# One core's fused image tokenizer, attention and expert block: the token product of the coming pair issued earlier on TensorE, into another bank, with the shared products and VectorE's list reordered

## The reference, cut to what matters

```python
tokens = einsum('bsd,hd->bsh', patches, W) + b      # 196 patches of 588 values
h = concat([cls, tokens], 1) + pos; h = concat([h, txt], 1)
x = layernorm(h)
...
total = gate * total + (1.0 - gate) * pos_contrib   # causal sums over the sequence
h = h + x + total / norm @ Wo + bo
x = layernorm(h)
scores = sigmoid(x @ gate_w.T)                      # top 2 of 64 experts, 256 places each
routed = sum over the 2 experts of (silu(x w1) * (x w3)) w2 * weight
shared = (silu(x @ sw1) * (x @ sw3)) @ sw2
h = h + shared + routed
```

## Time and profile before

| what | value |
|---|---|
| runs of the kernel before | 1828.45, 1853.2, 1863.95 us (median 1853.2) |
| profiled execution, first to last instruction (its span; no other time of that execution is listed) | 1823.6 us |
| TensorE matmul busy, share of the span | 84% |
| VectorE, ScalarE, GpSimd busy | 78%, 69%, 67% |
| mean granted TensorE clock | 0.956 of full |

### The profile page before, as it was taken

One profiled execution on the slowest core, in us unless ns is written; L12 is line 12 of the kernel. 1 busy time (PEld: TensorE's weight loads), 2 busy tenths in 40 slices (PEclk: granted clock), 3 DMA queues, 4 the chain that ended last, 5 costly groups with the idle time before them and its releaser, 6 DMA issues.

```text
span 1823.6 us, 30829 instructions
## 1 busy us (share of the span) xinstructions
PE 1534.0 (84%) x9237; PEld 1158.6 (64%) x9237; DVE 1421.6 (78%) x5705; ACT 1256.5 (69%) x2195; POOL 1226.0 (67%) x973
## 2 busy tenths in 40 slices
PE   2888998999899999888989898999889975676672
PEld 1566776777676767656767666677667764554552
DVE  3477997999797988777888888889888975587661
ACT  2897997988788878777878787889878851111110
POOL 1025776777676767666667676777667767488887
PEclk9899999999999999999999999999999998899886
DMA  9965666666666666556555655566656221476653
GB/s 182 229 138 120 138 139 125 123 121 124 102 117 100 117 101 106 96 103 103 95 101 104 108 102 102 101 111 105 103 103 103 63 59 40 96 116 109 98 88 35
DMA packets 267117, 197.21 MB, mean 108 GB/s; under 512 B 65464, under 2 KB 246437, under 8 KB 266953
## 3 DMA queue, kind: packets, MB, share of 16 engines
q1 hardware_dynamic: 210120, 174.84, 50.2%
q0 software_dynamic: 51200, 17.87, 8.4%
q10 hardware_dynamic: 5633, 2.56, 0.7%
HBM read 86.24 MB, written 85.39 MB: 94 GB/s over the span
## 4 chain that ended last, share of the span: by engine, by line
PE 40%; ACT 22%; issue 11%; POOL 9%; another core or an unknown queue 8%; DVE 7%; DMA 3%; SPq 0%; ACTq 0%; POOLq 0%; DVEq 0%
POOL out_rows L639 6%; PE bank L919 5%; PE bank L999 5%; ACT img L656 5%; ACT xh L739 4%; PE bank L1087 3%; PE bank L982 3%; POOL slot_rows L605 3%; PE bank L946 2%; PE bank L1018 2%; PE bank L1078 2%; ACT xs L726 2%; ACT kq L793 2%; ACT kq L792 2%
## 5 line engine op out<-in xcount | busy, mean ns | idle before, releaser
L605 POOL DMA_INDIRECT slot_rows<-xs,slot x768 | 874.1, 1138 | 284.5 <-issue 247.3
L656 ACT ACTIVATE img<-img 84x980 f32<-84x980 f32 x190 | 339.6, 1788 | 14.8 <-DMA img<-in_x 7.2
L591 POOL TENSOR_TENSOR rs<-ve,neg_half 128x12 f32<-128x12 f32 (+1 forms) x66 | 150.3, 2277 | 234.4 <-DVE ve L1342 232.8
L919 PE MATMUL bank<-img,w_tok 126*128 126x392 f32 (+1 forms) x640 | 228.7, 505 | 27.9 <-DMA img<-img 23.3
L639 POOL DMA_INDIRECT out_rows<-img,etok x128 | 198.7, 1552 | 64.0 <-issue 35.0
L919 PEld LDWEIGHTS bank<-img,w_tok 126*128 126x128 f32 (+1 forms) x640 | 124.0, 195 | 113.3 <-issue 23.3
L982 PEld LDWEIGHTS bank<-pos_a,v 128*128 128x128 f32 x768 | 145.4, 198 | 54.0 <-issue 10.8
L982 PE MATMUL bank<-pos_a,v 128*128 128x325 f32 (+2 forms) x768 | 163.8, 351 | 6.1 <-issue 3.8
L726 ACT ACTIVATE xs<-h,nb,rs 128x128 f32<-128x128 f32 x384 | 154.0, 481 | 3.0 <-DVE nb L1348 3.0
L739 ACT ACTIVATE xh<-h,nb,rs 128x128 f32<-128x128 f32 x384 | 154.0, 480 | 1.3 <-DVE nb L1348 1.3
L1499 DVE TENSOR_TENSOR h<-bank,hbo 128x768 f32<-128x768 f32 x64 | 61.1, 955 | 114.6 <-remote 103.3
(11 more groups left out here) (217 smaller groups left out, 3697.1 us busy)
## 6 DMA issues: line engine op xcount, KB each, us to landing
img<-in_x SPq DMA_DIRECT2D x384, 150.1 KB
img<-img SPq DMA_DIRECT2D x254, 160.8 KB
img<-img SPq DMA_DIRECT2D x128, 128.6 KB
out_rows<-fin SPq DMA_DIRECT2D x128, 128.0 KB
slot_rows<-xs,slot POOLq DMA_INDIRECT x768
slot_rows<-init_rows SPq DMA_DIRECT2D x16, 540.0 KB, 9.1
img<-slot_rows SPq DMA_DIRECT2D x32, 270.0 KB
h<-in_txt SPq DMA_DIRECT2D x64, 128.0 KB
```

What stands on the lines that cost most here:

```text
L591: g.tensor_tensor(out=rs[:, q.u, half:], in0=ve[:, q.u, half:], in1=neg_half[:, half:], op=ALU.pow).then_inc(S["p_rs"], 1)
L605: g.indirect_dma_start(out=slots_d, out_offset=bass.IndirectOffsetOnAxis(ap=slot[0:nt, q.x, r, part:part + 1], axis=0), in_=xs[0:nt, q.x, ...
L656: a.activation(cols[:, b0:b0 + nb, :], raw[:, q.u, :].rearrange("p (t b) -> p b t", b=P)[:, b0:b0 + nb, :], ACT.Copy)\
L919: ins = mm(bank[:, 5, 0:2 * PATCHES], w_tok[r, m, :], xk[r, k.u, :, m, :], start=(m == 0), stop=(m == SHIFT - 1))
```

## The change

- On TensorE `token(k)` moves from behind the shared products to right behind `position_out_1(p2)`. It writes bank 3 instead of bank 5, and waits for ScalarE's `angles` of pair k-2 (`a_th`), the reader of bank 3, instead of its gate.
- `shared_1a` and `shared_1b` come next, in that order, then `position_out_0`, then `shared_3a` and `shared_3b` into banks 4 and 5 (they were 3 and 4). The waits move with them: `shared_1a` waits for `v_h2`, `shared_3a` for `v_fin` and the gate, and `pe_f1a` (which ScalarE's SiLU waits for) is counted by `shared_1b`.
- `shared_out` waits for a new semaphore `v_su`, which `shared_product` counts, instead of `v_ht`. `products(w)` counts the pairs whose shared products are not put off. Where no further pair runs (the end of the first part) `shared_1a` and `counts` get a wait of their own.
- On VectorE `token_sum` moves in front of `block_pairs` and `score`; `weigh_position` moves from behind `indices` to behind `score`, and `shared_product` behind it, so that these two stand last before `residual_bias`.

No instruction with work in it is added or removed. The diff, cut to its core:

```diff
@@ token
-                wait(pe, S["a_g"], k, 2)
+                wait(pe, S["a_th"], k, 2)
...
-                    ins = mm(bank[:, 5, 0:2 * PATCHES], w_tok[r, m, :], xk[r, k.u, :, m, :],
+                    ins = mm(bank[:, 3, 0:2 * PATCHES], w_tok[r, m, :], xk[r, k.u, :, m, :],
@@ shared_out
-                wait(pe, S["v_ht"], w, -4)
                 if later(w):
                     tr(bank[:, 4, 0:TILE], ident, ident).then_inc(S["pe_o"], 1)
                     return
+                pe.wait_ge(S["v_su"], products(w))
@@ shared_1a
+                wait(pe, S["v_h2"], z, -1)
...
+                if not later(z):
+                    mm(bank[:, 0, 0:L], sw1[:, :], x2_t[:, 0, :], start=True, stop=True)
@@ shared_1b
-                wait(pe, S["v_h2"], z, -1)
...
+                    mm(bank[:, 1, 0:L], sw1[:, :], x2_t[:, 1, :], start=True, stop=True).then_inc(S["pe_f1a"], 1)
@@ shared_3a
+                    wait(pe, S["v_fin"], z, 1)
+                    wait(pe, S["a_g"], z, -2)
+                    mm(bank[:, 4, 0:L], sw3[:, :], x2_t[:, 0, :], start=True, stop=True)
@@ TensorE's body
                     gates(p2)
                     position_out_1(p2)
+                if k.runs():
+                    token(k)
+                    if first(k):
+                        position_products()
                 if p4.runs():
+                    shared_1a(p4)
                     shared_1b(p4)
                 if p2.runs():
                     position_out_0(p2)
                 if p4.runs():
                     shared_3a(p4)
                     shared_3b(p4)
-                    shared_1a(p4)
-                if k.runs():
-                    token(k)
-                    if first(k):
-                        position_products()
                 if p2.runs():
                     scores(p2)
@@ VectorE's body
                     indices(p4)
-                if p2.runs():
-                    weigh_position(p2)
                 if p4.runs():
                     one_hot(p4)
                     score_low(p4)
...
                 if p4.runs():
                     either(p4)
-                    shared_product(p4)
+                if k.runs():
+                    token_sum(k)
+                if p4.runs():
                     block_pairs(p4)
                     score(p4)
-                if k.runs():
-                    token_sum(k)
+                if p2.runs():
+                    weigh_position(p2)
+                if p4.runs():
+                    shared_product(p4)
                 if p2.runs():
                     residual_bias(p2)
```

More of the change, by code:

```diff
@@ L143, in first, with products @@
     return pair.c == 0
+def products(pair):
+    return pair.count() - sum(c <= pair.c for c in LATER)
 def steps(body, begin, end):
@@ L396, in program @@
              v_max v_lohi v_imax v_idx v_hot v_both v_bp v_cnt v_pick v_place v_over v_slot v_fin
-              v_sg  v_sinv
+              v_sg  v_sinv v_su
             a_d0 a_d1 a_d2 a_h a_xh a_xt a_th a_abs a_sin a_qs a_g a_x2 a_x2t a_lgt a_sl a_lg a_small
@@ L966, in counts @@
                 pe.wait_ge(S["v_bp"], w.count())
+                if not w.back(-2).runs():
+                    pe.wait_ge(S["a_sl"], w.count())
                 flat = both[:, :, :].rearrange("p t e -> p (t e)")
@@ L1021, in shared_3b @@
             def shared_3b(z):
-                wait(pe, S["v_fin"], z, 1)
-                wait(pe, S["a_g"], z, -2)
                 if later(z):
-                    tr(bank[:, 4, 0:TILE], ident, ident).then_inc(S["pe_f3b"], 1)
+                    wait(pe, S["v_fin"], z, 1)
+                    wait(pe, S["a_g"], z, -2)
+                    tr(bank[:, 5, 0:TILE], ident, ident).then_inc(S["pe_f3b"], 1)
                 else:
-                    mm(bank[:, 4, 0:L], sw3[:, :], x2_t[:, 1, :], start=True, stop=True).then_inc(S["pe_f3b"], 1)
+                    mm(bank[:, 5, 0:L], sw3[:, :], x2_t[:, 1, :], start=True, stop=True).then_inc(S["pe_f3b"], 1)
             def shared_1a(z):
[L1032 to L1035, removed]
+                wait(pe, S["v_h2"], z, -1)
+                if not z.back(-1).runs():
+                    wait(pe, S["v_fin"], z, 1)
+                if not later(z):
+                    mm(bank[:, 0, 0:L], sw1[:, :], x2_t[:, 0, :], start=True, stop=True)
             def logits(z):
@@ L1044, in shared_1b @@
             def shared_1b(z):
-                wait(pe, S["v_h2"], z, -1)
-                if not later(z):
-                    mm(bank[:, 1, 0:L], sw1[:, :], x2_t[:, 1, :], start=True, stop=True)
+                if later(z):
+                    tr(bank[:, 0, 0:TILE], ident, ident).then_inc(S["pe_f1a"], 1)
+                else:
+                    mm(bank[:, 1, 0:L], sw1[:, :], x2_t[:, 1, :], start=True, stop=True).then_inc(S["pe_f1a"], 1)
             def shared_3a(z):
                 if not later(z):
-                    mm(bank[:, 3, 0:L], sw3[:, :], x2_t[:, 0, :], start=True, stop=True)
+                    wait(pe, S["v_fin"], z, 1)
+                    wait(pe, S["a_g"], z, -2)
+                    mm(bank[:, 4, 0:L], sw3[:, :], x2_t[:, 0, :], start=True, stop=True)
             def transpose_1(k):
@@ L1352, in token_sum @@
                 dve.wait_ge(S["pe_tok"], k.count())
-                TT(h_t[:, :, 1:NIMG], bank[:, 5, 0:2 * PATCHES].rearrange("p (s t) -> p s t", s=2),
+                TT(h_t[:, :, 1:NIMG], bank[:, 3, 0:2 * PATCHES].rearrange("p (s t) -> p s t", s=2),
                    pos_t[:, 1:NIMG].rearrange("p (o t) -> p o t", o=1).to_broadcast([D, 2, PATCHES]), ALU.add)\
@@ L1485, in shared_product @@
                 if not later(z):
-                    TT(su[:, :, :], sl[:, :, :], bank[:, 3:5, 0:L], ALU.mult)
+                    TT(su[:, :, :], sl[:, :, :], bank[:, 4:6, 0:L], ALU.mult).then_inc(S["v_su"], 1)
             def top_values(z):
```

## The result

The changed kernel takes 1925.35 us (median of 4 runs, 1912.65 to 1936.81), the kernel before beside it 1857.35 us (4 runs, 1828.45 to 1863.95). The ratio is 1.043, with a 95% interval of 1.033 to 1.054: slower by 68 us where 38 were forecast. Ratios and their intervals leave out executions in a slower state of the chip, so a ratio is not the quotient of the two medians beside it. The profiled execution of the changed kernel has a span of 1923.2 us, 99.6 us more than that of the kernel before (1823.6); the two profiles lie further apart than the medians. Lines have moved: L924 is the token product (L919 before), L965 the scores (L960), L1510 the second sum (L1499), L1471 `weigh_position` (L1460), L1364 the token sum (L1353), L1089 the projection (L1078), L463 the spreads (L458).

What follows compares the result with a forecast made beforehand. TensorE (matmuls 92% busy in a middle stretch) and VectorE (85%) were taken to bound the kernel. Terms of 30 and 8 us gave 38, added to 1853.2: 1891 us, slower by 2.1%; range 1835 to 1935.

Steps and rivals of the forecast that it cites:

- L1048's idle time: TensorE's wait for the second sum before its first shared product, 30.2 us over the program; forecast to vanish.
- 25 pairs, 30 us: Token product in prompt pairs: waits 1.4 us for its patches, scores 1.4 us later; 1.2 us taken in 25 pairs.
- prompt: Pairs whose second sum on VectorE has no "remote" wait, 25 of 64; TensorE was said to have no gap there.
- late pair: One of 39 of 64 pairs whose second sum has a "remote" wait; the token product was to fill 2.29 us of waiting.
- The landing: Time from SP's last spread issue to the patches being there: 3.1 us, from one token product released by the DMA.
- remote: VectorE's wait before the second sum, 103.3 us, read as TensorE's counts coming late while SP issues; forecast near 100 us.
- rival A: Late counts before the second sum shrink: 60 us less, 1793 us, faster; sign "remote" under 60 us; chance 0.14.
- Scores 8.7 us behind the sum in late pairs: Forecast sign in the profile after: scores, waiting for `weigh_position`, start at 8.7 us instead of 7.80.
- forecast shift of 0.9 us: TensorE reaches its next projection 0.9 us later in late pairs, as scores wait for `weigh_position` in VectorE's new order.
- This VectorE step: VectorE's new order in late pairs: costs 0 to 0.9 us in each of 39, 0.2 taken, 8 us.
- B: Rival: no change; patches land by 906, the 0.9 us stays hidden behind SP; 8 us or less, about 1858; chance 0.26.
- C: Rival: much slower; patches land after 5 us, not 3.1, prompt pairs pay 3.3 us; 75 us, 1928 us; chance 0.14.

Runs made afterwards that it cites:

- before, profiled again: The kernel before, unedited, run and profiled again beside the experiments: 1793.87 us, ratio 1.00.
- after, profiled again: The changed kernel, unedited, run again beside the experiments: 1900.06 us, ratio 1.060 to the kernel before.
- wait filled: The changed kernel with three spare products on TensorE ahead of the token product's wait for its patches: 1841.28 us, ratio 1.027 to the kernel before.
- two of three early: The changed kernel with the spreads of the first two column chunks issued ahead of the store, the last chunk's behind it: 1850.97 us, ratio 1.033.
- early patches: The changed kernel with the third column chunk turned ahead of the shared SiLU and all spreads issued ahead of the store: 1808.44 us, ratio 1.009.
- token back, weigh first: The changed kernel with the token product in its old place and `weigh_position` ahead of the token sum, now behind `score`: 1800.89 us, ratio 1.001.
- `weigh_position` first: The changed kernel with early patches, and `weigh_position` ahead of `token_sum`, `block_pairs` and `score` on VectorE: 1809.58 us, ratio 1.006 to the kernel before.

## Why the prediction was wrong in its size

The pair, cut at VectorE's finished rows, the second sum and the scores, means over 55 pairs of the middle, worked out from the starts and ends in each timeline ("rows" are the finished rows, the end of `add_shared`):

| us per pair | rows to sum | sum to scores | scores to next rows | pair |
|---|---|---|---|---|
| before, first runs | 8.32 | 8.30 | 6.02 | 22.64 |
| after, first runs | 6.70 | 11.85 | 5.71 | 24.26 |
| before, profiled again | 7.42 | 8.66 | 5.92 | 22.00 |
| after, profiled again | 6.84 | 11.65 | 5.44 | 23.93 |
| wait filled | 6.22 | 11.20 | 5.54 | 22.96 |
| two of three early | 6.06 | 10.48 | 6.51 | 23.05 |
| early patches | 6.04 | 9.74 | 6.44 | 22.22 |
| token back, weigh first | 7.22 | 8.85 | 5.76 | 21.83 |

**Right.** The sign, the place and the releaser: the token product waits for its patches in the new place, TensorE's list behind it is late, and the scores come later behind the sum. The early patches take the wait away, and with it 1.060 becomes 1.009 (in another group of runs). L1048's idle time is gone as forecast (its successor L1043 has 0.7 us). The new bank and the new order of the shared products cost nothing that shows, as charged.

**Wrong: the term "25 pairs, 30 us".** This step failed in three ways, all in "the token product, prompt pairs".

- *The number of pairs.* I let only the pairs wait that I called prompt. In all 55 pairs the product waits. The trace of before had the answer: over 54 of its pairs the first position output ends 2.5 us behind SP's last spread in the mean (median 2.1), so that the 3.1 us of the earlier trace rows alone make 39 of the 54 wait, for 1.26 us each, 58 us over 64 pairs. One late pair had stood for all the late ones.
- *The landing.* 3.1 us came from one released product. In the changed kernel the token starts 4.06 us behind the last issue in the mean, 3.3 to 4.7 in eight pairs of ten. With 4.06 the same sum over the trace of before gives 108 us.
- *The clock.* No term of the sum held it. The product's busy time grew by 68 us, 625 ns against 505. Filling the wait shows what it is worth: 59 of the 106 us in that group of runs. The prediction treated a matmul's duration as fixed.

**Wrong the other way: what VectorE's waits give back.** Between the two first profiles, 99.6 us apart, the stretch from the sum to the scores grew by 3.55 us a pair, 227 us over 64 pairs. Of this, 104 us were given back from the finished rows to the sum: there a pair became 1.6 us shorter, and the "remote" wait before the sum fell from 103.3 to 40.9 us. This is rival A's place, its size of some 60 us and its sign in the profile (under 60 us); but A was forecast as the whole of the result and came as a discount. How much of it the change made stays open. Beside the experiments the stretch shrinks by 0.6 us, the kernel before has but 51.0 us of that wait, and there the change costs 106 us.

**The smaller terms.** "Scores 8.7 us behind the sum in late pairs" did not come about, since the token's wait delays them in all pairs (11.85 us in the mean). The forecast shift of 0.9 us shows only without that wait: with early patches they come at 9.74 us, 1.1 later than the 8.66 of the kernel before, profiled again, and `weigh_position` is what they mostly wait for. This VectorE step was forecast at 8 us; with the wait gone the ratio of 1.009 leaves 16 us for it and all else. `weigh_position` first did not lower that measurably, so what makes up the 16 us is not settled. Nothing here tells either why 22 of the 55 pairs keep the full clock; the waits of the 33 (mean 2.6 us) are only a little longer than those of the 22 (2.3 us).

**The rivals.** B (patches there by 906) and its 2.0 us of fixed time fell with the 4.06 us. C's mechanism, a later landing, was the nearest to what happened. Its price was put at 1928 us, against 1925 measured, by other terms: 25 waits of 3 us, where 55 of 2.5 and a low clock came, less A's discount. That the two times agree is chance.

## What to carry to other kernels

Before moving an operation ahead, take from the trace, for all pairs and not for one, how far its new place lies behind the issue that feeds it, and set that against the landing as it was seen; the operations that it jumps over were the cover. A wait of two microseconds on TensorE cost twice here: look at the granted clock around such a wait, and try whether harmless work in the wait gives the clock back. When a producer moves on one engine, the consumer's list on the other must be reordered with it, and the test of either half alone tells what the other half is for.

## What was not expected of the hardware

- Spare matmuls made a kernel faster: 1841 us with three extra products in each of 56 pairs, 1900 without.
- The clock fell late: in the 33 pairs of the changed kernel with a product of over 4 us, from 1.1 us before the product's start, at the end of the wait, to 1.2 us behind it, so that in 20 of them the product started at 1.00 and lost it afterwards. With waits of 1.1 us in the mean it held in 53 of 55 pairs.
- That TensorE's counts come late because SP issues, as the prediction had it, is not shown. With all six spreads ahead of the store the kernel before has 5.7 us of "remote" wait before the second sum instead of 51.0; with four of the six it has 78.9. The changed kernel with early patches has such a wait before `add_shared` (55.7 and 63.7 us), the kernel before with the same order on SP has not (1.6 us). The cause of the delay stays open.
- The same kernel before took 1857 us in the first runs and 1794 us beside the experiments, 3% less, and the change cost more there (1.060 for 1.043).
